# Ten identity products of 512 columns in TensorE's three pauses of a top-2 routing

## The reference

```python
x = x + tanh(g_xattn[0]) * L0_xattn(layernorm(x), ctx)        # 32 query heads on 8 key heads
x = x + tanh(g_ffn[0])   * L0_ffn(layernorm(x))               # base product and low-rank experts
x = x + tanh(g_xattn[1]) * L1_xattn(layernorm(x), ctx)
x = x + tanh(g_ffn[1])   * L1_ffn(layernorm(x))

def L1_ffn(x, W_gate, b_gate, W_e, b_e):                      # W_gate 512x8, W_e 8x512x512
    logits = x @ W_gate + b_gate
    _, top_idx = top_k(logits, 2)
    y_all = relu(einsum('bsd,edh->bseh', x, W_e) + b_e)
    y = take_along_axis(y_all, top_idx[..., None], axis=2)
    return y.mean(axis=2)
```

## Time and profile before

| | us |
|---|---|
| median of 3 runs | 953.14 (952.55 to 953.42) |
| the profiled execution | 953.01 |
| its span, first to last instruction | 951.2 |
| TensorE busy in it | 885.7 |
| mean granted clock of TensorE | 0.955 |

### The profile page before, as it was taken

One profiled execution on the slowest core, in us unless ns is written; L12 is line 12 of the kernel. 1 busy time (PEld: TensorE's weight loads), 2 busy tenths in 40 slices (PEclk: granted clock), 3 DMA queues, 4 the chain that ended last, 5 costly groups with the idle time before them and its releaser, 6 DMA issues.

```text
span 951.2 us, 13808 instructions
## 1 busy us (share of the span) xinstructions
PE 885.7 (93%) x4739; PEld 721.5 (76%) x4739; DVE 616.2 (65%) x1061; ACT 324.5 (34%) x581; POOL 415.8 (44%) x423
## 2 busy tenths in 40 slices
PE   5999999999999999999999999998999999667993
PEld 4778878977878887877887877766799995655772
DVE  6975674376575366576446577677898865876345
ACT  5333133224133214214214214231566773612230
POOL 4651442153352153153243162337888616537551
PEclk9999999999999999999999999999899995569997
DMA  9020120020120011111002002031255306323448
GB/s 315 14 89 1 34 89 1 12 82 8 34 89 1 14 45 45 34 45 45 12 11 79 1 1 79 1 113 39 65 170 154 89 5 228 133 67 115 140 143 310
DMA packets 42242, 70.13 MB, mean 74 GB/s; under 512 B 7034, under 2 KB 14779, under 8 KB 42051
## 3 DMA queue, kind: packets, MB, share of 16 engines
q1 hardware_dynamic: 37060, 56.97, 18.5%
q0 software_dynamic: 3680, 12.06, 3.9%
q10 hardware_dynamic: 1440, 0.24, 0.1%
HBM read 52.61 MB, written 10.22 MB: 66 GB/s over the span
## 4 chain that ended last, share of the span: by engine, by line
PE 80%; DVE 9%; DMA 3%; issue 3%; ACT 1%; POOL 1%; SPq 1%; ACTq 0%; DVEq 0%
PE ps L1373 17%; PE ps L1375 16%; PE ps L1374 16%; PE ps L1494 6%; PE ps L1486 6%; PE ps L1623 6%; PE ps L1611 3%; PE ps L1502 3%; DMA rows_in<-h_rows,gather_i 2%; PE ps L1604 2%; PE ps L1672 1%; DMA rb<-in_router_b 1%; DVE h L922 1%; DVE stats L916 1%; PE ps L1718 1%
## 5 line engine op out<-in xcount | busy, mean ns | idle before, releaser
L528 POOL TENSOR_TENSOR q_t<-rot_a,rot_b 128x512 f32<-128x512 f32 x64 | 82.6, 1291 | 152.7 <-DVE rot_b L967 152.7
L965 DVE TENSOR_TENSOR rot_a<-ps,cos 128x512 f32<-128x512 f32 x80 | 55.2, 689 | 87.3 <-PE ps L1375 86.7
L1373 PE MATMUL ps<-xt_hi,wq_hi 128*128 128x512 f32 x256 | 107.6, 420 | 0.5 <-DVE rot_b L967 0.5
L1373 PE MATMUL ps<-wo_hi,at_hi 128*128 128x512 f32 x256 | 106.7, 417 | 0.4 <-DVE at_lo L1073 0.4
L1375 PE MATMUL ps<-xt_hi,wq_lo 128*128 128x512 f32 x256 | 101.1, 395 | 0.0
L1374 PE MATMUL ps<-xt_lo,wq_hi 128*128 128x512 f32 x256 | 101.0, 394 | 0.0
L1375 PE MATMUL ps<-wo_hi,at_lo 128*128 128x512 f32 x256 | 100.2, 391 | 0.0
L1374 PE MATMUL ps<-wo_lo,at_hi 128*128 128x512 f32 x256 | 99.8, 390 | 0.0
L760 ACT ACTIVATE ps<-ps 128x512 f32<-128x512 f32 x64 | 37.2, 582 | 178.6 <-PE ps L1486 178.6
L773 ACT ACTIVATE at_hi<-ps 128x512 fp32r<-128x512 f32 x64 | 38.2, 597 | 171.5 <-PE ps L1502 171.5
L1078 DVE TENSOR_TENSOR X<-ps,X 128x512 f32<-128x512 f32 x64 | 44.2, 690 | 73.9 <-PE ps L1375 73.6
(11 more groups left out here) (218 smaller groups left out, 2125.7 us busy)
## 6 DMA issues: line engine op xcount, KB each, us to landing
wq_raw<-in_wq SPq DMA_DIRECT2D x8, 1024.0 KB, 5.4
wo_raw<-in_wo SPq DMA_DIRECT2D x8, 1024.0 KB, 5.1
w_raw<-in_we SPq DMA_DIRECT2D x8, 1024.0 KB, 5.7
X<-in_x SPq DMA_DIRECT2D x4, 512.0 KB, 13.1
wk_raw<-in_wk SPq DMA_DIRECT2D x8, 256.0 KB, 2.9
q_t<-in_ctx_t SPq DMA_DIRECT2D x2, 1024.0 KB, 9.9
wv_raw<-in_wv SPq DMA_DIRECT2D x4, 512.0 KB, 3.8
ctx_s<-in_ctx SPq DMA_DIRECT2D x8, 256.0 KB, 4.7
```

The costliest lines, as they stand in the source:

```text
L528: nc.gpsimd.tensor_tensor(dst, rot_a[:, r % 2, :], rot_b[:, r % 2, :], ALU.add).then_inc(rope_ok, 1)
L965: nc.vector.tensor_tensor(heads(rot_a[:, r % 2, :]), heads(bank), bcast(cos[:, :], 4), ALU.mult)
L1373: nc.tensor.matmul(dst, w_hi, x_hi, start=start and k == 0, stop=False)
```

## The change

A helper `keep_warm(n)` is added to TensorE's block. It issues n products with `ident` as the stationary operand and the 512 columns of `X[:, 0, :]` streaming, into bank 7, whose content nobody reads before it is overwritten. They wait for no semaphore and raise none. Three stand between the last gate and the waits of L1703, two between the rank products and the list products, five between the list products and `turn_in(0)`.

```diff
             gate(B - 1)
 
+            def keep_warm(n):
+                for _ in range(n):
+                    nc.tensor.matmul(ps[:, 7, :], ident[:, :], X[:, 0, :], start=True, stop=True)
+
+            keep_warm(3)
             pe.wait_ge(kz_ok, CREDIT + 1)
             pe.wait_ge(tri_ok, CREDIT + 1)
             pe.wait_ge(sel_ok, CREDIT + 2)
...
             last.then_inc(rank_mm, 1)
+            keep_warm(2)
             for n in range(B * TOP):
                 if n % KT == 0:
                     pe.wait_ge(hot_ok, CREDIT + n // KT + 2)
...
+            keep_warm(5)
             turn_in(0)
             pe.wait_ge(slot_ok, CREDIT + 25)
```

## The result

The changed kernel takes 949.73 us in the median of 12 runs (945.6 to 954.15), and the kernel before, timed beside it, 952.79 (950.24 to 954.7, 12 runs): 3.1 us less, a ratio of 0.9972 with a 95% interval of 0.9959 to 0.9984. Its profiled execution took 950.80 us with a span of 949.0.

The account below looks back on a forecast made before the run. TensorE's clock stood at half from 787.6 to 848.20 us, with pauses waiting on VectorE and GpSimd. Terms -0.45 + 0 + 0.8 - 1.7 = -1.35, then -1.5 at expert 6, about -2.8 from 953.1: 950.3 us, range 948.6 to 953.9.

Parts of the forecast that it names:

- The slow rival: In the pauses, added f32 products do not lift the clock: 3.6 us slower, 956.7 us; chance 0.10.
- the row that spoke for it: Ahead of the routing, six 65-row, 512-column records of L1672 stream 5.33 us from 787.63 without a clock rise.
- my three places: Streaming before earlier clock rises: 3.7 us at kernel start, 2.9 at the first expert, 3.5 from 872.0.
- the term: Third pause, ahead of `turn_in(0)`: five products take 6.1 us, 0.8 us too long, so 0.8 lost.
- where I put nothing: Second pause, two products: they cost nothing, the clock falls again before the list products, gain 0.
- the terms: Pauses ahead of the first tile: 0.45 us gained in the first, 0 in the second, 0.8 lost in the third.
- Expert 0: From `turn_in(0)` to the first expert's end, transposes and products at full level: gain 1.7 us.
- The dip: At expert 6, near 872, the clock's fall to half goes once work is earlier: another 1.5 us gained.
- the second half of the forecast: At expert 6, the half-level stretch disappears: 1.5 us gained, leaned to but not certain.
- the first sum: Three pauses and the first expert together: -0.45 + 0 + 0.8 - 1.7 = -1.35 us.
- the rival with the clock up in the list: Clock stays up through the list products, the five hidden: 3.25 us faster, 949.9 us; chance 0.12.

Follow-up runs that it names:

- 65 rows: The changed kernel with its ten products using 65 rows of the identity and of X instead of 128: 955.27 us, ratio 1.0033.
- four in the second pause: The changed kernel with four instead of two products between the rank and the list products: 949.47 us, ratio 0.9975.
- transposes: The changed kernel with each of its ten products replaced by eight f32 transposes of 128 columns of X: 948.79 us, ratio 0.9968.
- eight for five: The changed kernel with eight instead of five products ahead of the first tile's transposes: 953.06 us, ratio 1.0006.
- the kernel with single products ahead of the routing: The changed kernel plus three single 512-column identity products before the gate loop and one of 256 columns in each of its eight steps: 942.78 us, ratio 0.991.

## Why the prediction was right, step by step

**The level and the price.** The products raised the clock as assumed, and an f32 product costs 1.70 us at half and 0.86 at full. The slow rival was a real one: with 65 rows it came out, at 955.3 instead of its 956.7, and the forecast was right to hold the height against the row that spoke for it (65 rows streaming without a rise).

**The rise came later than taken.** I took 3.7 us after the first product. In the full change it came 4.8 us after it both times (823.50 to 828.3, 837.23 to 842.0), and over all profiled executions with full-height work in the pauses 3.0 to 5.4. Of my three places, the one at the first expert was read too short: TensorE had been at full-height transposes since 842.65, 5.5 us ahead of the rise, and I had left these out. So the three products ran at half nearly to their end and still let L1708 start 0.33 us after `sel`, as before. The five took 6.75 instead of 6.1 us: a loss of 1.2 to 1.4 us where the term was 0.8.

**The list products gained where I put nothing.** `slot` came 0.29 us earlier, not 0.45, as `n_e` waited 0.73 instead of 0.58 us for a first rank product just behind the helper. But the level fell only at 835.1, 0.8 us into the sixteen, which with their start by VectorE brought the list 0.79 us earlier in all, not 0.45. That the two misses nearly cancel is luck: the first tile starts 16.10 us after `sel`, before 15.65, which is 0.45 later, and the terms said 0.35.

**Expert 0.** 843.98 to 849.03 is 5.05 us, before 6.85: 1.80 gained, 1.7 predicted. The sum at its bias is 22.83 - 21.47 = **1.36 us**, predicted 1.35, and the table shows at least as much in what follows (3.59 us at expert 22's bias, 1.56 of it the dip).

**The dip.** Expert 6 gained 1.56 us between the two profiled executions, predicted 1.5, but my reason was wrong. I argued that the fall's instant would stay and the work would move away from it. Instants do not stay: the fall ahead of the gate loop came at 786.8 before and at 794.2, 785.6, 787.1 and 784.6 in later kernels whose code up to there is the same. In the full change the idle is even longer (2.50 us) and no fall follows; with only the five, behind 2.68 us, it does. The dip was there in six of eleven profiled kernels, at no one length of the idle, so whether an execution has it looks like chance, in the kernel before as in the changed one. No run shows that it is rarer in the changed kernel, and the sum should not have counted it whole. So the second half of the forecast, 1.5 of its 2.8 us, came true in the one profiled pair by luck, and the medians cannot be said to contain it.

The shown part of the gain is the 1.36 us at expert 0's bias. Of the 3.61 us at expert 6's, the dip is 1.56, and another 0.7 us lies in waits for rows and weights, which I had not priced and which the single profiles show in both directions. The medians moved by 3.1 us, with an interval of 1.5 to 3.9, so the 1.4 of the first sum lies just below it; where the rest of the 3.1 comes from stays open.

**The range.** The twelve runs of one kernel spread over 3.6 to 8.6 us. The predicted 950.3 lies 0.6 over the median, and the 949.9 of the rival with the clock up in the list is nearer still (0.2); the profile says that it was not that rival, with 0.50 granted from 0.8 us into the list products on. The number alone would not have told them apart.

## What to carry to other kernels

Where TensorE waits for another engine's chain and granted clock reads 0.50 behind the wait, full-height products into an unread bank are worth trying, but each such block has two prices, at half and at full, and the one just ahead of work on the critical path must fit its pause at the price that it will really run at. Look first for the longest half-level stretch in which TensorE itself is the path: here the 35 us ahead of the routing gave about 8 us (941.18 against 949.73), and the three pauses 3. Several profiles, or the spread of the times, are needed before a single dip is put into a sum.

## What the runs showed of the hardware

- TensorE was busy for 8.5 to 8.7 us without a break, with products 65 rows high or 8 columns wide, and the granted clock stayed at 0.50. With 128 rows in the same places, as 512-column products or as 128-column transposes, it was at 1.00 from 3.0 to 5.4 us after the first of them.
- At expert 6 a fall came with idles of 2.14 us (before) to 2.74 us (four in the second pause), and none with 2.48 us (transposes) to 2.84 us (65 rows). With 2.48 us it went either way: eight for five has a fall, transposes none.
- With idles of 1.03 and 1.17 us next to the 65-row products of L1672 (L1679 there), the level fell in the one profiled execution of the kernel with single products ahead of the routing; by the mean granted clock (0.976 to 0.983 against 0.965 and 0.968), eight of its ten runs kept the level for most of that stretch.
